# Attention layers 1 and 2 of a diffusion block: memsets moved behind the first layer norm, and unread full-array products added to the fill and the last iterations

## The reference

```python
x_norm = _ln(x) * (1 + scale_a) + shift_a          # 16 heads of 8 channels
q, k, v = split(x_norm @ W_qkv + b_qkv)
x = x + gate_a * (softmax(q k^T * 8 ** -0.5) v @ W_proj + b_proj)
q = _ln(x) @ W_qc + b_qc
k, v = split(context @ W_kvc + b_kvc)              # 77 context rows; layer 1 normalises them first
x = x + softmax(q k^T * 8 ** -0.5) v @ W_cproj + b_cproj
```

## Time and profile before

| engine | busy us | share | instructions |
|---|---|---|---|
| PE | 3103.4 | 86% | 31983 |
| PEld | 2065.1 | 57% | 31983 |
| DVE | 2810.7 | 77% | 12664 |
| ACT | 2171.0 | 60% | 5124 |
| POOL | 1200.7 | 33% | 1534 |

### The profile page before, as it was taken

The page is one execution under the profiler, slowest core; times in us unless marked ns, Lnnn a source line. Parts: engine busy times, 40 slices in busy tenths (PEclk is TensorE's granted clock), DMA queues, the critical chain, the costliest instruction groups (busy, mean ns, idle before and its releaser), DMA issues. The chain is left out here.

```text
span 3629.3 us, 94366 instructions
## 1 busy us (share of the span) xinstructions
PE 3103.4 (86%) x31983; PEld 2065.1 (57%) x31983; DVE 2810.7 (77%) x12664; ACT 2171.0 (60%) x5124; POOL 1200.7 (33%) x1534
## 2 busy tenths in 40 slices
PE   3999967777777769789999997879999998879999
PEld 2454534444444437556666664646666665558887
DVE  5677759999999978578887766858887774966665
ACT  1566645555555647557776665637776664646665
POOL 2000026666666656521122213531112211532221
PEclk9999978889888879889999987969999996979999
DMA  4000000000000000034444430024444441000000
GB/s 130 12 13 13 13 9 8 8 8 9 6 8 8 6 2 1 21 97 107 106 106 104 105 82 3 1 76 106 106 108 100 104 104 29 1 23 10 13 13 16
DMA packets 135426, 162.87 MB, mean 45 GB/s; under 512 B 40742, under 2 KB 85414, under 8 KB 134566
## 3 DMA queue, kind: packets, MB, share of 16 engines
q1 hardware_dynamic: 114182, 121.62, 13.5%
q0 software_dynamic: 12160, 26.04, 3.1%
q10 hardware_dynamic: 8608, 9.18, 1.0%
HBM read 13.81 MB, written 4.19 MB: 5 GB/s over the span
## 5 line engine op out<-in xcount | busy, mean ns | idle before, releaser
L1253 ACT ACTIVATE attn_pT<-attn_t 128x512 f32<-128x512 f32 (+1 forms) x1024 | 555.5, 596 | 335.4 <-PE attn_t L1509 334.6
L1370 DVE TENSOR_REDUCE attn_mx<-attn_s 128x4 f32<-128x512 f32 (+1 forms) x1024 | 549.6, 579 | 152.8 <-PE attn_s L1494 151.3
L636 ACT ACTIVATE topk_prob<-topk_s,topk_nmx 128x77 f32<-128x77 f32 x1024 | 248.3, 326 | 319.7 <-POOL topk_nmx L532 213.2
L1494 PEld LDWEIGHTS attn_s<-packed_keys,packed_queries 32*128 32x128 f32 x4096 | 282.9, 193 | 164.1 <-DVE attn_mx L1370 97.1
L1175 POOL DMA_DIRECT2D packed_queries<-attn_om x256 | 142.7, 557 | 662.9 <-ACT attn_om L1246 659.2
L1494 PE MATMUL attn_s<-packed_keys,packed_queries 32*128 32x128 f32 (+1 forms) x4096 | 348.4, 291 | 14.3 <-DVE attn_mx L1370 6.2
L1534 PE MATMUL attn_o<-attn_pT,attn_vp 128*18 128x128 f32 (+1 forms) x8192 | 336.5, 284 | 0.0
L538 POOL TENSOR_SCALAR topk_mask<-topk_work 128x308 f32<-128x308 f32 x256 | 252.9, 988 | 224.5 <-DVE topk_work L779 222.5
L1509 PE MATMUL attn_t<-packed_queries,packed_keys 32*128 32x128 f32 (+1 forms) x4096 | 306.0, 268 | 1.8 <-ACT attn_pT L1253 1.8
L927 PE MATMUL topk_t<-ident,topk_prob 128*77 128x128 f32 x1024 | 187.3, 313 | 138.5 <-POOL topk_prob L542 138.1
L927 PEld LDWEIGHTS topk_t<-ident,topk_prob 128*77 128x77 f32 x1024 | 139.7, 171 | 250.3 <-issue 140.7
(11 more groups left out here) (309 smaller groups left out, 7780.0 us busy)
## 6 DMA issues: line engine op xcount, KB each, us to landing
packed_queries<-attn_qT SPq DMA_DIRECT2D x720, 64.0 KB, 2.2
packed_keys<-attn_kT SPq DMA_DIRECT2D x384, 64.0 KB, 2.1
packed_queries<-attn_om POOLq DMA_DIRECT2D x256, 64.0 KB, 2.4
packed_queries<-zero_rows SPq DMA_DIRECT2D x120, 128.0 KB, 2.7
packed_keys<-attn_kT SPq DMA_DIRECT2D x384, 39.0 KB, 2.1
kbd<-window_kT SPq DMA_DIRECT2D x512, 8.0 KB
kbd<-topk_kT SPq DMA_DIRECT2D x512, 4.8 KB
weights<-in_weights ACTq DMA_DIRECT2D x1, 3524.5 KB, 14.6
```

The costliest lines, as they stand in the source:

```text
L636: last = nc.scalar.activation(prob[:, u % 4, h * keys:(h + 1) * keys], s_ps[:, u % 2, h * keys:(h + 1) * keys], ACT.Exp, scale=SCALE, bias ...
L1253: nc.scalar.activation(pT[0:keys, c % 2, h, :], t_ps[0:keys, h, :], ACT.Exp, scale=SCALE).then_inc(s_exp, 1)
L1370: nc.vector.tensor_reduce(mx[:, (c // 2) % 2, 2 * k + h, :], sc, AX.X, ALU.max).then_inc(s_max, 1)
L1494: last = nc.tensor.matmul(s_ps[:, h, k * KW:(k + 1) * KW], r.qp[32 * j:32 * j + 32, buf, k, b * T:(b + 1) * T], r.kp[32 * j:32 * j + 32, b ...
```

## The change

It is made in `packed_attention_layer`, and so applies to layers 1 and 2.

1. POOL runs `rstd_of(0)` first and the four memsets after it. DVE's wait for `s_init` moves from the start of its prologue to just before `values_out(0)`.
2. PE's waits for `s_zero` and `s_init` move behind its prologue. A function `unread(count)` issues products of the shape of `keep_clock`'s, from buffer 2 of the packed keys into the bank f_ps. The prologue issues ten of them before it waits for anything, and four after each of the four PE operations of groups 0 and 1: 42 a layer.
3. In the body a second branch issues `keep_clock(i, m3, 2)` where no `UNREAD` count applies, the group i + 2 doesn't exist, and scores or transposed scores are computed: u = 4 to 7 of iterations 30 and 31, u = 0 to 6 of iteration 32, 30 products a layer.

```diff
         @block.gpsimd
         def _(pool):
+            def rstd_of(g):
...

+            rstd_of(0)
             nc.gpsimd.memset(vp[:, :, :, :, :, :, :], 0.0).then_inc(s_init, 1)
...
             def prologue():
-                rstd_of(0)
                 rstd_of(1)
                 pack_queries(pool, 0, 0)
...
             def prologue():
-                dve.wait_ge(s_init, n_init)
                 ln_stats(0)
...
                     ln_apply(g + 1)
+                    if g == 0:
+                        dve.wait_ge(s_init, n_init)
                     values_out(g, g)
...
+            def unread(count):
+                for _ in range(count):
+                    nc.tensor.matmul(f_ps[:, :], r.kp[:, 2, 0, 0:T], r.kp[:, 2, 0, :], start=True, stop=True)
+
             def prologue():
+                unread(10)
+                for g in range(2):
+                    transpose_xn(g)
+                    unread(4)
+                    project_keys(g)
+                    unread(4)
+                    project_queries(g)
+                    unread(4)
+                    project_values(g)
+                    unread(4)
                 pe.wait_ge(s_zero, 1)
                 pe.wait_ge(s_init, n_init)
-                for g in range(2):
-                    transpose_xn(g)
-                    project_keys(g)
-                    project_queries(g)
-                    project_values(g)
...
                     if now and u < len(UNREAD):
                         keep_clock(i, m3, UNREAD[u])
+                    elif not there(before, left, 2) and (now or back):
+                        keep_clock(i, m3, 2)
```

More of the change, by code:

```diff
@@ L1161, in _ @@
         def _(pool):
[L1162 to L1167, removed]
             def rstd_of(g):
@@ L1184, in stage_context @@
                                source[:, G * q:G * q + G, :]).then_inc(s_ctx, 16)
+            rstd_of(0)
+            nc.gpsimd.memset(vp[:, :, :, :, :, :, :], 0.0).then_inc(s_init, 1)
+            pool.wait_ge(s_init, 1)
+            nc.gpsimd.memset(vp[:, :, :, :, :, 0, D:D + 1], 1.0).then_inc(s_init, 1)
+            nc.gpsimd.memset(vp[:, :, :, :, :, 1, 2 * D + 1:2 * D + 2], 1.0).then_inc(s_init, 1)
+            nc.gpsimd.memset(ctxs[:, :].rearrange("c (b s) -> c b s", s=KW_C)[:, :, S:KW_C], 0.0
+                             ).then_inc(s_init, 1)
             def prologue():
-                rstd_of(0)
                 rstd_of(1)
```

## The result

| kernel | median us | range | runs |
|---|---|---|---|
| before | 3639.03 | 3634.42 to 3642.21 | 5 |
| after | 3612.0 | 3594.9 to 3625.12 | 5 |

The ratio of after to before is 0.9926, 95% interval 0.9901 to 0.9951: faster by 27 us, with a spread of 30 us between the runs of the changed kernel. Its profiled execution is the slowest of them, 3625.1 us (span 3623.3, mean clock 0.929; before 3631.1, 3629.3 and 0.918). So this one trace shows 6 us of the 27, and the first task is to see where it differs from the others.

A forecast was written before the change was run, and what follows sets the result against it. Bound at a layer's start: one chain with PE at half clock; at its end: PE itself, slow by its clock. Start 18.2 plus tail 24.4 is 42.6 us; from the 3640.8 median, 3598 to 3594, predicted 3596, range 3576 to 3620.

The forecast's parts named there:

- Tail: Iterations 30 to 32 and the chain behind: gain 14.1 us in layer 1, 10.3 in layer 2, together 24.4.
- the clock doesn't answer to products where PE is busy anyway: Rival on the layers' ends: added products don't move the clock and only cost; 3642 us, the same; chance 0.04.
- I take no stretch: Group 0's normalisation beside the 3 us memset keeps its length, so the gain stays 2.8 us a layer.
- The row with the memset disagrees: Four normalising instructions took 1.11 us beside a 0.52 us POOL memset, read as contradicting the skill's exclusion rule.
- the memset blocks the normalisation: Rival in the fill: normalisation stands until the memset is over, 2.8 us lost twice, 3602 us; chance 0.12.
- The whole clock from about 1520 until the scores: Sign of being right, in the fill: granted clock 1.00 from about 1520 until the scores.
- 5.3 us forecast in the fill: Gain a layer from unread products in the fill: 6.8 - 0.5 - 0.1 - 0.9 us.
- I expect the whole clock between the last of the ten and the first transposes: In the fill, the clock returns before group 0's transposes; 0.5 us a layer charged for the still slow part.
- the packing of the queries: On POOL's queue, still 0.5 to 1 us ahead of the scores; rival: too late, 3599 us, chance 0.04.
- Iteration 0: Two steps at the whole clock gain 1.0 us, ends 0 and 6.5; rival: whole clock kept, 3585 us, chance 0.08.
- Start together: Start of each layer: 2.8 + 5.3 + 1.0 = 9.1 us gained; both layers, 18.2.
- A time that moved in the phases between: Sign of being wrong: a changed time in phases between the edges, which nothing in the change touches.

The follow-up runs named there:

- part 3 alone: Kernel before plus only the pairs of unread products in iterations 30 to 32: 3609.1 us, ratio 0.9941.
- part 2 alone: Kernel before plus only PE's prologue with its 42 unread products, memsets first as before: 3626.3 us, ratio 0.9990.
- the gated kernel: Changed kernel plus a POOL wait for the first normalisation before its memsets: 3594.1 us, ratio 0.9906; run again 3597.2 us, ratio 0.9907.
- part 1 alone: Kernel before with only the memsets behind the first power and DVE's wait moved, no unread products: 3629.4 us, ratio 1.0001.

## Why the prediction was right or wrong

The prediction was 3596 us, from 3576 to 3620; the medians are 3612.0 and, run again beside its variants, 3603.7. Direction and range hold. The forecast itself is 8 to 16 us low, and not for one reason.

**Tail: right, with its sizes.** Iteration 31 was put at 17.5 us in both layers and took 17.66 in both; in every trace that has part 3 it took 17.64 to 17.66, and 18.18 where keep_clock's counts were raised too. Six steps of iteration 32 were put at 12.0 and took 12.41. The last projection is at half speed again (2.08 us, as before), as was said. 24.4 us were forecast, 26.0 are in the trace, 21.4 in the medians of part 3 alone. The rival "the clock doesn't answer to products where PE is busy anyway" is dead: at 0.50 PE was busy 20.20 of 20.20 us, and with two more products in each of the steps that had none the same iteration runs at 1.00 with PE busy 17.45 of 17.66, and is at 1.00 in all 18 layers traced with part 3. What it gives depends on what the clock would have done without: 18.93 to 26.41 us in the six layers traced, so 1.3 to 8.8 us an iteration. The Trainium skill ("TensorE: Matmul & The Clock Gate", "HAM oscillation — how this bites in real kernels") explains the fall by gaps in which PE idles. These rows disagree: the longest that PE idled in iteration 30 before the fall at 2156.2 was 0.57 us, and at 0.50 it didn't idle at all.

```profile
2155.18 0.27 PE L1494 MATMUL attn_s<-packed_keys,packed_queries 32*128 32x78 f32 x1 [0.57 <-ACT attn_pT L1253]
```

**Part 1: wrong, in the step "I take no stretch".** Of two rows that disagreed I took the memset of 0.52 us beside an unstretched normalisation, as the nearest because it was a memset. The other end held: 3.56 us instead of 1.12. And the near row was misread. It adds up four instructions; the first of them alone, in the kernel before and then in the changed one:

```profile
1348.36 0.44 DVE L1759 TENSOR_SCALAR mlp_xn<-x_res,mlp_mv,mlp_rstd 128x128 f32<-128x128 f32 x1 [0.25 <-POOL mlp_rstd L1706]
```

```profile
1519.04 2.97 DVE L1336 TENSOR_SCALAR attn_xn<-x_res,attn_mv,attn_rstd 128x128 f32<-128x128 f32 x1 [1.12 <-POOL attn_rstd L1164]
```

One such instruction takes 0.34 to 0.35 us with POOL idle. The first ended at 1348.80, 0.08 us behind the short memset's end (1348.72); the second at 1522.01, 0.08 us behind the long one's (1521.93). Both stood until the memset was over; the short one had only 0.36 us left when DVE began, so almost nothing showed in the sum of four. The prediction's "The row with the memset disagrees" is wrong. The rule of the Trainium skill ("SBUF — State Buffer", "Who interferes with whom"), that such a DVE instruction and one of GpSimd exclude each other as a whole, fits all of these rows, and 1.12 us as soon as the memset waits. The rival "the memset blocks the normalisation" was given 0.12 and 2.8 us a layer. Its mechanism was right, its price too low: holding the memsets back gave 2.5 to 5.0 us in the fill, because a blocked normalisation also leaves PE idle for 3.14 us and the first keys at half speed.

**Part 2: the clock came back, but later than forecast, and the gain did not.** Ten products of 3.57 us and 1.12 us for the queries of group 0 came as forecast. The whole clock from about 1520 until the scores did not: it was there from 1527.4, with 3.4 us at 0.50 from 1541.1. But of 5.3 us forecast in the fill, 1.4 are in part 2 alone. Two steps failed. First, "I expect the whole clock between the last of the ten and the first transposes": in layer 1 it came only behind the keys; in layer 2 the transposes ran at the whole clock (0.66 us) and the keys no longer did (1.97). Without the memset in the way transposes and keys both had it in two of the four layers of the gated kernel's traces. Second, the chain was followed only to the packing of the queries. A faster group 1 runs into the packing of group 0's keys: ACT waits 3.31 us for it. With part 1 alone, where the fill stays slow, ACT is held there by PE and not by the DMA:

```profile
1543.31 0.69 ACT L1228 ACTIVATE attn_kT<-attn_l,bias_cols 128x512 fp32r<-128x512 f32 x1 [2.25 <-PE attn_l L1471]
```

In the gated kernel it waits for the DMA once more (2.85 to 3.51 us). From the low keys of group 0 to the keys of group 1 pass 10.6 to 12.2 us in all 18 layers traced with part 2, 12.28 before. The packing ends this stretch, and a faster PE no longer shortens it. What lies before and behind it still follows the clock, so that the fills with the memsets held back take 25.67 to 27.76 us. From group 0's transposes to the first scores 19.2 us were forecast instead of 25.05; it took 23.1 to 24.2 in the changed kernel's traces and 21.5 to 23.7 in the gated one's.

**Iteration 0: a size.** 1.0 us was taken between 0 and 6.5; 1.5 came (23.76 to 22.27), and iteration 1 lost 0.7 us in layer 1 and gained 0.4 in layer 2. The upper end is real, 5.4 us for iteration 0 and some 2.4 for iteration 1, but takes more than this change does.

**Start together:** 18.2 forecast, 7.2 measured, 11 short. 42.6 - 11 + 1.6 of the tail = 33.2 us, which is 3597.9 for the profiled execution without its middle. The medians show 27.0 and 28.9.

**The middle: not in the sum at all.** "A time that moved in the phases between" was named as a sign of error. All that lies outside the two attention layers lost 2.1 us together, but iterations 2 to 29, which nothing here touches either, lost 25.1. The runs show that it comes and goes: absent in the changed kernel's second trace, present in part 3 alone in layer 1, ahead of any added product. All three long falls (30.8, 30.8 and 17.1 us) stand right behind a packing DMA for which ACT waited 1.91 to 2.38 us. But of the eight such waits of 1.9 us and more between iterations 2 and 29 of all traces four had only 3.4 us of half clock at once behind them, and one none. So a late packing goes with the long falls and doesn't decide them; what does stays open, and that the DMA causes the fall was not tried. That the medians lie 4 to 6 us short of 33.2 would fit a fall in some executions of both kernels; with one or two traces each that is argued, not shown. The kernel before spreads as well, 22 us in 23 runs, and its slower runs have the lower mean clock, 0.913 to 0.920; 0.007 of 3630 us is some 50 us at half clock (an estimate from these two). The clock isn't all of the spread: the changed kernel's runs of 3594.9 and 3612.7 us both have 0.935. A profiled execution must be compared stage by stage.

## What to carry to other kernels

A tail whose PE is busy all the time can still stand at half the clock. Here two unread full-array products in each step that had none gave back 8.7 us of a 26.3 us iteration; beside a trace in which the clock had come back by itself it would be 1.3; whether smaller products would do it was not tried. Further products in steps already at the whole clock cost 0.15 us each. Work moved "behind" the critical instruction must be held there by a wait, or it lands beside it: here the normalisation began 3.0 us earlier and lost 2.4 of them beside a long memset. And where a chain is made shorter, look at every transfer that frees a buffer of that chain, not only at the one that its end waits for.

## What the runs showed of the hardware that I had not expected

- Four DVE normalisations of 128x128 took 3.56 us beside a POOL memset of 128x3456, and 1.12 us in the changed kernel once the memset waited; a variance of 128x4 took 1.83 us beside it and 0.17 alone. A normalising instruction ended 0.08 us behind the memset's end, beside the long memset and beside one of 0.52 us: it stood for as long as the memset had left.
- After PE had stood idle for 1.93 us behind a late packing DMA, its clock stayed at 0.50 for 30.5 us with PE busy 30.20 of them; a second kernel shows the same behind 1.51 us, 30.24 of 30.5. Keep_clock's full-array products in half of the steps did not end it sooner. Idle times of 1.62 and 1.63 us in layer 2 of two other traces had none and 3.4 us at 0.50 behind them.
- In iteration 0 the clock fell 4.7 us in with products in every step of it, and kept 1.00 with the same products where the fill had more of them. Up to the fall PE was equally busy in both; the first 4.7 us of the one that fell, then of the one that held:

```profile
1546.91:1551.60 4.69, 3.72 (x32) 2.55 (x31) 2.75 (x5) 0.00 (x0) 4.69 (x10) 1.00 0.78 221
```

```profile
1546.09:1550.80 4.71, 3.74 (x32) 2.57 (x31) 2.75 (x5) 0.00 (x0) 4.71 (x10) 1.00 0.75 225
```

  How busy PE was in the iteration up to there did not decide it. The first had stood at 0.50 from 1541.3 to 1544.7, just before the scores, the second had been at 1.00 since 1526.5; but layer 2 of the second kernel had no such fall either and fell in iteration 0 all the same.
